# Moving three of the four output-projection parts, and the aggregation behind them, to later periods of the plain attention

## The reference, cut to what matters

```
q, k, v = src @ Wq + bq, src @ Wk + bk, src @ Wv + bv      # 16 heads of 16
probs   = softmax(q k^T * scale)
attn    = (probs v) @ Wo + bo                               # the output projection
x       = layer_norm(src + attn, ln1_g, ln1_b)
expert_idx = floor(x @ router_w + router_b) mod 4
y       = relu(x @ W1[e] + b1[e]) @ W2[e] + b2[e]           # for the row's expert e
out     = layer_norm(x + y, ln2_g, ln2_b)
```

## Time and profile before

| what | us |
|---|---|
| median of three runs | 1988.62 |
| lowest and highest | 1988.22, 1990.94 |
| the profiled execution | 1989.43 |
| its span | 1987.7 |
| busy: PE, PE weight load, DVE, ACT, POOL | 1784.8, 1061.6, 1316.7, 827.5, 980.9 |
| mean granted clock of TensorE | 0.941 |

### The profile page before, as it was taken

The page is one execution under the profiler, slowest core; times in us unless marked ns, Lnnn a source line. Parts: engine busy times, 40 slices in busy tenths (PEclk is TensorE's granted clock), DMA queues, the critical chain, the costliest instruction groups (busy, mean ns, idle before and its releaser), DMA issues.

```text
span 1987.7 us, 32178 instructions
## 1 busy us (share of the span) xinstructions
PE 1784.8 (90%) x11513; PEld 1061.6 (53%) x11514; DVE 1316.7 (66%) x2934; ACT 827.5 (42%) x1140; POOL 980.9 (49%) x631
## 2 busy tenths in 40 slices
PE   5989989989987299995699999999999999999998
PEld 2333434334333299995455656556565465554654
DVE  5767787887876377775765666657656477565760
ACT  2645555655644044442153251442524424244242
POOL 1134354354255244444357385473863737737464
PEclk7889988988988699998799999999999999999999
DMA  6547536537542555554100100101001010010100
GB/s 113 91 128 138 87 111 139 92 108 136 86 159 95 228 207 211 215 213 134 41 2 1 44 1 11 33 1 43 1 12 33 2 43 1 9 35 1 33 1 11
DMA packets 81440, 151.52 MB, mean 76 GB/s; under 512 B 11638, under 2 KB 55318, under 8 KB 75420
## 3 DMA queue, kind: packets, MB, share of 16 engines
q1 hardware_dynamic: 77980, 141.12, 27.2%
q0 software_dynamic: 3072, 8.39, 1.3%
q10 hardware_dynamic: 256, 0.26, 0.1%
HBM read 84.47 MB, written 39.85 MB: 63 GB/s over the span
## 4 chain that ended last, share of the span: by engine, by line
PE 42%; POOL 4%; DVE 3%; issue 1%; ACT 1%; DMA 0%; POOLq 0%; DVEq 0%; SPq 0%
PE a_psO L729 12%; PE a_psS L715 11%; PE a_psO L752 6%; PE a_psM L689 5%; PE a_psS L677 4%; PE a_psS L742 3%; POOL a_k_tok L362 2%; POOL a_q_tok L362 2%; PE a_psS L661 2%; ACT a_probs L480 1%; DVE a_junk L546 1%; POOL a_oT L385 1%; DVE a_alibi L623 0%; DVE a_qL L536 0%; DVE a_turned L554 0%
## 5 line engine op out<-in xcount | busy, mean ns | idle before, releaser
L397 POOL TENSOR_TENSOR a_probs<-a_probs 128x1024 f32<-128x1024 f32 x144 | 341.8, 2402 | 300.1 <-PE a_psO L729 300.1
L546 DVE CUSTOM_DVE_ANT_0 a_junk<-a_psM,a_alibi 128x512 bf16<-128x512 f32 x512 | 333.3, 689 | 198.9 <-PE a_psM L689 195.6
L1330 DVE TENSOR_REDUCE f_n_tok<-f_psR 128x1 f32<-128x512 f32 x512 | 324.9, 682 | 99.6 <-PE f_psR L1563 97.3
L480 ACT ACTIVATE a_probs<-a_psS 128x1024 f32<-128x1024 f32 x256 | 248.9, 1024 | 271.4 <-PE a_psS L715 270.7
L1274 ACT ACTIVATE f_probs<-f_psS 128x1024 f32<-128x1024 f32 x256 | 247.9, 1023 | 189.1 <-PE f_psS L1582 187.6
L729 PE MATMUL a_psO<-a_probs,a_v 128*32 128x512 f32 x2048 | 244.0, 597 | 0.0
L1563 PE MATMUL f_psR<-f_kP,f_qP 48*128 48x512 f32 x512 | 163.6, 538 | 48.6 <-DVE f_n_tok L1330 34.1
L1563 PEld LDWEIGHTS f_psR<-f_kP,f_qP 48*128 48x128 f32 x512 | 65.1, 201 | 231.1 <-issue 105.9
L1595 PE MATMUL f_psO<-f_probs,f_v 128*32 128x512 f32 x1024 | 150.6, 663 | 0.3 <-ACT f_probs L1274 0.3
L689 PE MATMUL a_psM<-a_kH,a_qH 64*128 64x512 f32 x512 | 122.6, 474 | 29.0 <-DVE a_n_tok L546 28.8
L1142 POOL TENSOR_TENSOR f_oT<-f_oT,f_rsum 128x512 f32<-128x512 f32 x31 | 39.7, 1281 | 201.9 <-DVE f_rsum L1343 201.9
(11 more groups left out here) (212 smaller groups left out, 3547.4 us busy)
## 6 DMA issues: line engine op xcount, KB each, us to landing
w_w_high<-w_parts SPq DMA_DIRECT2D x23, 1024.0 KB, 5.4
w_w_low<-w_parts SPq DMA_DIRECT2D x23, 1024.0 KB, 7.5
sorted_rows<-f_zeros SPq DMA_DIRECT2D x6, 1408.0 KB, 5.6
f_kP<-f_high SPq DMA_DIRECT2D x64, 128.0 KB, 5.6
f_qP<-f_high SPq DMA_DIRECT2D x64, 128.0 KB, 7.3
f_w_raw<-in_L_ffn_W SPq DMA_DIRECT2D x16, 512.0 KB, 5.4
w_parts<-f_w_high SPq DMA_DIRECT2D x16, 512.0 KB, 2.7
w_parts<-f_w_low SPq DMA_DIRECT2D x16, 512.0 KB, 4.3
```

The source lines that it names most:

```text
L397: nc.gpsimd.tensor_tensor(slots, slots, probs[:, first - GRP:first - GRP + 2, :], ALU.add).then_inc(added.sem, 1)
L480: nc.scalar.activation(probs[:, slots, :], psS[:, 2 * p:2 * p + 2, :], ACT.Exp).then_inc(exp_done.sem, 1)
L546: nc.vector.tensor_tensor_reduce(out=junk[:, a, :], in0=psM[:, a, :], in1=alibi[:, h, :], scale=1.0, scalar=-3.0e38, op0=ALU.add, op1=ALU.max,
L1330: nc.vector.tensor_reduce(n_tok[:, c, column:column + 1], psR[:, ring_bank("max", batch, u), :], AX.X, ALU.max, negate=True).then_inc(max_ ...
```

## The change

The second, third and fourth part of the output projection move from periods 9, 11 and 12 to 10, 12 and 14; the first stays in period 8. The aggregation of their statistics on VectorE moves from period 12 to period 14. `LAST_EXTRAS`, the POOL's list and SyncE's list stay as they are.

```diff
@@ plain_attention_phase
     EXTRAS = {(0, 1): [("maxima", 1), ("v", 1)], (1, 0): [("proj", 0)], (1, 1): [("maxima", 2), ("proj", 1)],
-              (1, 2): [("proj", 2)], (1, 3): [("proj", 3)], (2, 0): [("out", 0)], (2, 1): [("maxima", 3), ("out", 1)],
-              (2, 3): [("out", 2)], (3, 0): [("out", 3)], (3, 1): [("maxima", 0)], (3, 3): [("v", 0)]}
+              (1, 2): [("proj", 2)], (1, 3): [("proj", 3)], (2, 0): [("out", 0)], (2, 1): [("maxima", 3)],
+              (2, 2): [("out", 1)], (3, 0): [("out", 2)], (3, 1): [("maxima", 0)], (3, 2): [("out", 3)],
+              (3, 3): [("v", 0)]}
@@ the vector engine's batch
-                    if more and before and at == (3, 0):
+                    if more and before and at == (3, 2):
                         norm1.aggregate_rows(dve, b - 1)
```

## The result

The changed kernel takes 2013.72 us (median of four runs, 2011.71 to 2017.24), the kernel before 1988.42 beside it. The ratio is 1.0148, 95% interval 1.0129 to 1.0167: 1.5% slower; the two medians themselves lie 25.3 us apart. The profiled execution took 2017.24 us with a span of 2015.5, 27.8 above the span before; it is the slowest of the four.

What follows compares the result with a forecast made beforehand. TensorE and VectorE pace each other, with POOL nearly late (4.6 us of slack). Cycles of 44.81 + 7.8 + 0.9 + 23.7 = 77.2 us against 73.5 put batch 7's "out" 24.5 us later: 2013 us, range 2003 to 2026.

Steps and rivals of the forecast that it cites:

- the sum: Whole kernel: the profiled 1989.43 us plus 24.5 us gives 2013.9, stated as 2013 for a median.
- The later start of POOL's block: Batches 1 to 6: the block waits for the last "out" part and starts 7.8 us later, ends 7.0 to 10.5.
- its lower end: Period 10 gains an "out": 4.26 us forecast, with 3.89 as lower end, taken from batch 0's empty period 10.
- the floor named for period 11: Scores of period 12 need the transfer of period 9's maxima; period 11 lasted 6.31 us in batch 0.
- The floor of 23.7 us: POOL delivers the next batch's 1/sqrt(var) 23.7 us behind its block's start: 22.63 + 1.03 + 0.04.
- The wait at L128: Period 2 of the next batch: VectorE waits about 6 us for POOL's 1/sqrt(var), arriving 17.7 us behind the block's start.
- The clock behind the wait: From L128 to POOL's block: the lower clock behind the wait costs 0.9 us per batch.
- Rival (c): Behind the wait at L128: the lower clock costs 3.3 us each time, not 0.9; 2025 us, chance 0.14.
- the prediction's estimate of 3.5 us: Clock penalty per batch by the skill page's formula, for 7 us at the lower clock; total an estimated 2026 us.
- The tail: Batch 7: the block of batch 6 starts 26.4 us later, the first "out" waits for normalize(6, 3), +24.5 us.
- Rival (a): Period 8 to next batch: 2.7 us shorter in six batches if POOL delivers within 17.7 us; 1972 us, chance 0.06.
- Rival (b): No change, 1989 us: wait at L128 only about the 2.7 us gained, if block 20.4 or slip 4.5 us; chance 0.06.

Runs made afterwards that it cites:

- e12_change_again: The changed kernel as it is, run again beside later follow-up kernels as their measure: 2016.09 us, ratio 1.0179 to the kernel before.
- e2_last_part_back: Against the kernel before, only the second part moves, from period 9 to 10; the last part and the aggregation stay in 12: 1979.39 us, ratio 0.9977.

## Why the prediction was right

The forecast was 2013; the medians give 2013.7. The mechanism was the one forecast: POOL's block starts later, and L128 waits for what stands behind it. That the number fits within 1 us is partly luck, as two terms were wrong in opposite directions and the profiled execution lies 3 us above the sum. The steps one by one:

- The later start of POOL's block: 7.8 us forecast, 7.2 measured in batches 2, 3, 4 and 6. Period 10 took 3.90 (its lower end), 11 took 3.71 for 3.6, 13 took 4.11 for 4.13, and the block started 3.86 us into period 14 for 4.21. In batches 1 and 5 the start slipped by 10.9 and 8.9. In batch 1 that is the floor named for period 11: the scores of period 12 waited 1.15 us for the transfer of the maxima, and the clock fell. The clock fell in batch 5 too, at the same place; in the second profile of the same kernel (`e12_change_again`) it fell in batch 6 instead.
- The floor of 23.7 us from the block's start to L128: 23.6 to 23.7 in all five batches, and moved to 20.3 by shortening the block.
- The wait at L128: 6 forecast, 3.9 to 5.5 measured. The rest of the time was there, but further ahead: period 15 was put at about 6 us and took 6.45 at full clock and 7.7 to 7.9 where the clock fell. From the start of the batch VectorE was at L128 after 11.7 us, as forecast, though norm0's L106 was held for 0.9 to 1.8 us by POOL. As forecast, what lies between the block and L128 is hidden, so the error cost nothing.
- The clock behind the wait: 0.9 forecast. L128 to the block takes 53.0 to 54.3 us in undisturbed batches, less 44.81 and 7.2 that is 1.0 to 2.3. The term was too small by 0.8 us on average and the delay too large by 0.6: that they nearly cancel is luck. The cycle came out at 77.8 for 77.2, and most of the difference is batch 5. Rival (c), 3.3 us each time, was not what happened.
- By the Trainium skill, page "TensorE: Matmul & The Clock Gate", section "HAM oscillation — how this bites in real kernels", the penalty is the time at the lower clock times (1 - 1.2/2.4), which gave the prediction's estimate of 3.5 us. The traces disagree on the price here: 1.0 to 2.3 us.
- Why 0.9 was too small: it came from the whole stretch of batch 1 of the kernel before, and that batch isn't built like the others. These are periods 3, 4 and 5 and the start of 6, in batch 1 and in batch 4 (timeline of ACT of the kernel before):

```profile
136.38 1.94 ACT L1274 ACTIVATE f_probs<-f_psS 128x1024 f32<-128x1024 f32 x2 [1.23 <-PE f_psS L1582]
145.39 1.94 ACT L1274 ACTIVATE f_probs<-f_psS 128x1024 f32<-128x1024 f32 x2 [0.57 <-PE f_psS L1582]
150.72 1.94 ACT L1274 ACTIVATE f_probs<-f_psS 128x1024 f32<-128x1024 f32 x2
155.83 1.94 ACT L1274 ACTIVATE f_probs<-f_psS 128x1024 f32<-128x1024 f32 x2
...
361.33 1.94 ACT L1274 ACTIVATE f_probs<-f_psS 128x1024 f32<-128x1024 f32 x2 [1.23 <-PE f_psS L1582]
365.63 1.94 ACT L1274 ACTIVATE f_probs<-f_psS 128x1024 f32<-128x1024 f32 x2 [0.15 <-PE f_psS L1582]
370.75 1.94 ACT L1274 ACTIVATE f_probs<-f_psS 128x1024 f32<-128x1024 f32 x2
376.93 1.94 ACT L1274 ACTIVATE f_probs<-f_psS 128x1024 f32<-128x1024 f32 x2
```

  Periods 3 and 4 take 14.34 us in batch 1 and 9.42 in batch 4. Less the wait of 3.38 us that is 1.5 us for the clock, and not 0.9: period 5, which is 1.1 us shorter in batch 1 (5.11 for 6.18), had hidden part of it. The same reckoning gives 1.1 to 2.4 us in batches 2 to 6 of the changed kernel.
- The tail: the block of batch 6 was 30.0 us late (26.4 forecast), the "out" 27.3 (24.5), as the last chunk's data came 0.7 us sooner behind the block's start. Of the 3.6 us between 30.0 and 26.4, 2.8 come from the five cycles; the other 0.8 us are batch 1, whose start the prediction took as unchanged but for the 7.8 us. The profiled execution is thus 3 us above the sum; the medians of the runs, on which the forecast stood, moved by 25.3.
- Rival (a) held in part for its own stretch: periods 8 to 15 did get shorter in most batches (by 1.4 us in batch 4, by 2.9 in batch 2, for 2.7 forecast). What failed was its condition. With POOL's block apart, the placement of the change came to 12 us under the kernel before, but the wait for L106 had a part in that, and the placement wasn't the better one.
- Rival (b) named a block of some 20.4 us as its condition for no change. With the first `split_chunk` ahead of it the block was shorter than that (20.25 us from L1121 to L128, L89 included), and the kernel was still 0.6% slower than the kernel before.

What the prediction didn't see is that the wait for L89 has a twin in the port: had POOL delivered in time by taking up the variance earlier in its block, L128 would still have been held by the rest of the block. That took a run to see.

## What to carry to other kernels

Moving work to emptier slots moves everything that waits for its last piece. Follow the last piece across the engines: here a POOL block as long as a third of a batch stood behind it, and the next batch's variance at that block's end. An engine's slack is not its idle time but the distance from the end of its longest unbroken block to whoever needs the result; here 4.6 us on an engine idle half of the time.

## What the runs showed of the hardware

- A vector `tensor_scalar` from SBUF to SBUF was held until the POOL instruction beside it ended: 0.17 us became 1.78 (L106 beside L1120), a pair of 0.73 became 2.76 (L128 beside L1173). Maxima, which read PSUM, keep their 0.68 us beside L1173 (L1333 in that run). With an order between L106 and L1120, it is 0.17 again.
- In the kernel before, a stall of 1.6 us on VectorE was followed by some 10 us at 1.2 GHz in each of batches 1 to 6; without it the clock was 1.00 over the same periods. The whole was worth 0.64% of the kernel (0.41 to 0.87%).
- The stall doesn't bring the fall each time. With the last part back in period 12 and the second in 10, the same L106 took 1.78 us in every batch, and behind it the clock stayed full in batch 2 and was at 1.2 GHz for 3.4 to 10 us in the others (timeline of DVE and windows view of `e2_last_part_back`, batch 2):

```profile
253.88 1.78 DVE L106 TENSOR_SCALAR f_norm_var_eps<-f_norm_aggr 128x4 f32<-128x4 f32 x1
...
core 0: us, PE busy (x) PEld busy (x) DVE busy (x) ACT busy (x) POOL busy (x), PEclk, DMA share, GB/s
253.20:265.00 11.80, 9.60 (x56) 4.04 (x53) 11.04 (x21) 6.39 (x7) 11.25 (x8) 1.00 0.45 140
```

  The runs of the kernel before differ in the same way: 1971.21 us at a mean clock of 0.951, 1989.94 at 0.940.
